# Up and down convolution on fewer weight matrices, with column-shifted copies written by ScalarE

## The chip, the cores and the metric

The kernel runs on one core of a Trainium2 chip. The metric is the device time of one launch in microseconds; the median of several launches counts. TensorE (PE) multiplies, VectorE (DVE), ScalarE (ACT) and GpSimd (POOL) work on what it leaves in PSUM, SyncE (SP) issues DMAs. Each engine runs its own instructions in order, and semaphores tie the engines together.

## The reference

16 images of 32 x 32 pixels and 32 channels pass through a group norm, a convolution branch (added to the input), attention over the 1024 tokens of each image (added), and an expert-choice feed-forward layer (added). The change lies in the convolution branch:

```python
x = x + bias
x = jnp.repeat(jnp.repeat(x, 2, axis=2), 2, axis=3)      # up by 2
x = _conv_same(x, up_filter)                             # 12 x 12 low pass
x = jax.nn.leaky_relu(x, negative_slope=0.2) * sqrt(2)
x = _conv_same(x, dn_filter)                             # 12 x 12 low pass
x = x[:, :, ::2, ::2]                                    # down by 2
```

The filters work on each channel by itself, and both are separable; the kernel convolves along one image axis by the weights of a matrix product and along the other by adding up products over shifted data.

## The kernel before, in words

An image of a channel lies on TensorE's 128 partitions as four blocks of 32 (a block holds every fourth column, R = 4), and each partition holds 256 numbers: 32 rows `h` of JW = 8 columns `j`. A shift by one of those eight columns is a move by one `j`. Values are held as two float16 parts, high and low, so every weight matrix is multiplied three times (high x high, high x low, low x high).

`up` of image n makes four quarters of the upsampled image, each of 256 columns in PSUM (psB). A quarter t takes the weight matrices UU at index 4k - t + 6 for k = -1, 0, 1 where that index lies in 0 to 9; k is also the shift by which the image is read. k = 0 is a product of 256 columns; k = -1 and k = 1 leave out the column that falls off the edge and are products of 32 x 7 = 224 columns. That makes 1 + 1, 1 + 2, 1 + 2 and 1 + 1 matrices, so 10 matrices and 30 products, 12 of 256 columns and 18 of 224. `down` sums in one PSUM range (psA) the products of DD with the four quarters in `y`: also 10 matrices and 30 products, 12 of 256 and 18 of 224. Both go through `convolve` (line 892), unshifted products first.

The order of everything is written out by hand. `STEP` (line 133) is a list of events; in step t an event `batch(5, "up")` works on image t + 5, and so on. `schedule()` walks t from -9 to 21, and every engine walks the same list `EVENTS` and does its own part of each event. In step t stand, in this order: `prob` 0 of image t, `yQ` of t + 2, `pv` of t - 1, `prob` 1, `score` 0, `up` of t + 5, `prob` 2, in some steps work of a group of four images (`image`, `mean`, `uT`, `pool`), `shift` of t + 1, `down` of t + 4, `prob` 3 and 4, `zK` of t + 3, `tok` of t + 4. So image 4 goes through `down` in step 0, and images 0 to 3 in steps -4 to -1, where no attention runs yet.

On ACT an event of `up` is two activations out of PSUM (`y` high in float16 at line 557, `y32` at line 560), `prob` an exponential (line 587), `tok` three copies (lines 563 to 569), `yQ` one copy (line 578) whose low half DVE makes (line 752), `mean` squares (line 598), `image` two copies to float16 (line 553); `image_low` is DVE's part of the images (line 698), `y_low` POOL's (line 499). PSUM is two sets of four banks, each handed out in a ring by `place`: a unit on PE waits until the unit that had its banks has been read out.

Of the kernel before, what the change touches and what calls it, by code (L numbers as in the profile page):

```python
# [16 lines left out]
P = 128  # L17
# [23 lines left out]
HOMES = 4  # L41
SLOT = 1024
# [67 lines left out]

def span_of(n, i):

    return ((0, 2), (2, 3), (3, 4))[i] if n == G - 1 else ((0, 2), (2, 4))[i]
# [20 lines left out]
        once(-8, "xT", 3), batch(0, "prob", 0), group(6, "logit_max"), batch(2, "yQ"), batch(-1, "pv"),  # L134
# [6 lines left out]
        batch(4, "down"), once(-2, "image", 1), once(-3, "small", 2),  # L141
# [58 lines left out]
def hybrid_kernel(nc, x, bias, up_filter, dn_filter, Wq, Wk, Wv, gate_w, gate_b, weight1, weight2, out):  # L200
# [9 lines left out]
    with ExitStack() as ctx:  # L210
# [13 lines left out]
        xin = sb("xin", [P, 2, SLOT])  # L224
        biasr = sb("biasr", [P, H])
# [13 lines left out]
        y = sb("y", [P, 2, SLOT])  # L239
        w1_halves = sb("w1_halves", [P, SLOT])  # L240
# [101 lines left out]
        UU_ready, UU_copied = sem("UU_ready"), sem("UU_copied")  # L342
# [49 lines left out]

        def zV_count(n):

            return zV_loaded[n % HOMES], 16 * R * (n // HOMES + 1)

# [7 lines left out]
        def _(sp):  # L404
# [61 lines left out]
        def _(pool):  # L466
# [6 lines left out]
            nc.gpsimd.memset(pooled[:, :, :], 1.0).then_inc(fills_ready, 1)  # L473
            pool.wait_ge(power_ready, 1)
# [48 lines left out]
        def _(act):  # L523
# [20 lines left out]
            for e in EVENTS:  # L544
# [3 lines left out]
                if name == "image":  # L548
                    if n >= 2:
                        act.wait_ge(b_filled, BU["up", GB * (n - 1) - 1] + 1)  # L550
                    for i, (lo, hi) in enumerate(PIECES):
                        act.wait_ge(xin_sum, 2 * n + 1 + i)
                        nc.scalar.activation(img[n % 2][0][:, lo:hi], x_all[:, n, lo:hi], ACT.Copy).then_inc(xin_high, 1)
                if name == "up":
# [24 lines left out]
                elif name == "prob":  # L579
                    if n == 0:  # L580
                        act.wait_ge(UU_ready, 16 * 2)
                        act.wait_ge(UU_copied, 2)
# [42 lines left out]
        def _(dve):  # L625
# [19 lines left out]
            for e in EVENTS:  # L645
# [70 lines left out]
                elif name == "dnT":  # L716
# [156 lines left out]
        def _(pe):  # L873
# [15 lines left out]
            def convolve(out_cols, matrices):  # L889

                for i, (m, v, shift) in enumerate(sorted(matrices, key=lambda a: a[2] != 0)):
                    ins = nc.tensor.matmul(within(out_cols, -shift), m, within(v, shift), start=i == 0, stop=i == len(matrices) - 1)  # L892
# [18 lines left out]
            for e in EVENTS:  # L911
# [34 lines left out]
                elif name == "up":  # L946
# [6 lines left out]
                    parts = [v[:, BC * (n % GB):BC * (n % GB) + BC] for v in img[n // GB % 2]]  # L953
                    for t in range(R):
                        ins = convolve(s[:, BC * t:BC * t + BC],
                                       [(UU[:, i, R * k - t + NS - 1, :, :], parts[j], k) for k in (-1, 0, 1) if 0 <= R * k - t + NS - 1 < SPAN
                                        for i, j in ((0, 0), (0, 1), (1, 0))])
                elif name == "down":

                    pe.wait_ge(y_ready, n + 1)  # L960
                    if n == 0:
                        pe.wait_ge(a_drained, A["dnT", 0] + 1)
                    ins = convolve(s[:, 0:BC], [(DD[:, i, R * k + t + 3, :, :], y_parts[n % 2][j][:, BC * t:BC * t + BC], k) for k in (-1, 0, 1)
                                                for t in range(R) if 0 <= R * k + t + 3 < SPAN for i, j in ((0, 0), (0, 1), (1, 0))])
# [134 lines left out]
```

## Time and profile before

| | us |
|---|---|
| median of 3 runs | 368.54 (368.35 to 369.02) |
| the profiled execution | 368.35 |
| its span, first to last instruction | 366.5 |
| PE busy | 327.2 (89%) |
| DVE busy | 260.1 (71%) |
| ACT busy | 183.9 (50%) |
| POOL busy | 128.8 (35%) |

The profiled execution is the lowest of the three runs. Its time is the span and 1.85 us around it. All sums are made against the 368.35 us of that execution, which lies 0.19 us below the median. An instruction's duration in a row includes the way through the engine, so that neighbours on PE and ACT overlap; the pace of an engine is read from starts.

### The profile page before, as it was taken

To read this page: it belongs to the slowest core of one execution; us is meant where nothing else is said; L and a number is where in the kernel's file an instruction comes from. 1 tells how busy PE (TensorE), PEld (TensorE's weight loads), DVE (VectorE), ACT (ScalarE), POOL (GpSimd) and SP (SyncE) were. 2 spreads that over 40 slices of the span, in tenths; PEclk is the share of its full clock that TensorE was granted. 3 is DMA by queue.
4 is the path that set the end of the run, shared out by engine and by line. 5 is a ranking of instruction groups with operands and counts; after the bars stand their busy time and mean duration, and the time that the engine had idled before them with its cause. 6 is when DMAs were issued, how large, how long until landed. Compare 5 with 4: busy or idle time off the path is not lost.

```text
span 366.5 us, 8381 instructions
## 1 busy us (share of the span) xinstructions
PE 327.2 (89%) x3362; PEld 249.3 (68%) x3362; DVE 260.1 (71%) x523; ACT 183.9 (50%) x251; POOL 128.8 (35%) x96
## 2 busy tenths in 40 slices
PE   2289998799999999999899999999996986979985
PEld 1168886587777878786678787777774544546774
DVE  2679779957757877869686876776988786454632
ACT  1043355446557574757663755576564547440500
POOL 6134535332444337554211557312235400351000
PEclk9999999999999999999999999999999899995655
DMA  4910100001011010101000101011021100100122
GB/s 125 204 36 3 26 19 16 16 16 31 16 18 26 5 32 2 31 4 32 15 16 2 31 15 17 17 16 26 7 58 32 31 2 18 28 2 29 57 75 69
DMA packets 35906, 11.16 MB, mean 30 GB/s; under 512 B 24431, under 2 KB 35741, under 8 KB 35869
## 3 DMA queue, kind: packets, MB, share of 16 engines
q1 hardware_dynamic: 33152, 9.98, 11.3%
q10 hardware_dynamic: 2717, 0.66, 1.2%
q8 instruction: 27, 0.44, 0.5%
q14 instruction: 10, 0.08, 0.1%
HBM read 5.72 MB, written 4.21 MB: 27 GB/s over the span
## 4 chain that ended last, share of the span: by engine, by line
PE 77%; DVE 10%; DMA 5%; issue 3%; ACT 2%; POOL 1%; ACTq 1%; SPq 0%; DVEq 0%; POOLq 0%
PE psB L892 14%; PE psA L892 13%; PE psB L1025 9%; PE psB L1005 8%; PE psA L990 7%; PE psA L1070 4%; PE psA L882 3%; PE psA L1048 3%; PE psB L1039 3%; DVE negmax L757 2%; PE psA L993 2%; PE psA L983 2%; PE psA L1032 2%; PE psB L1008 2%; PE psB L977 2%
## 5 line engine op out<-in xcount | busy, mean ns | idle before, releaser
L757 DVE TENSOR_REDUCE negmax<-psA 128x1 f32<-128x512 f32 (+7 forms) x128 | 90.5, 751 | 32.2 <-PE psA L993 31.6
L587 ACT ACTIVATE Pp<-psB 128x1024 f32<-128x1024 f32 (+1 forms) x80 | 73.6, 937 | 35.3 <-PE psB L1008 30.7
L892 PE MATMUL psB<-xin,UU 128*128 128x224 f16 (+1 forms) x480 | 56.4, 277 | 0.1
L892 PE MATMUL psA<-y,DD 128*128 128x224 f16 (+1 forms) x480 | 55.1, 273 | 0.0
L990 PE MATMUL psA<-zK,yQ 128*128 128x512 f16 (+1 forms) x192 | 47.8, 332 | 6.0 <-DVE uT L775 2.4
L892 PEld LDWEIGHTS psB<-xin,UU 128*128 128x128 f16 x480 | 47.0, 99 | 7.9 <-DVE xin L698 0.5
L1005 PE MATMUL psB<-yQ,zK 128*128 128x512 f16 (+1 forms) x192 | 47.3, 330 | 3.7 <-DMA yQ<-rows 2.4
L892 PEld LDWEIGHTS psA<-y,DD 128*128 128x128 f16 x480 | 46.7, 98 | 5.5
L477 POOL TENSOR_TENSOR zrstd<-zrstd,power 128x8 f32<-128x8 f32 x16 | 27.2, 1698 | 53.9 <-DVE zrstd L735 53.9
L557 ACT ACTIVATE y<-psB 128x1024 f16<-128x1024 f32 x16 | 16.4, 1023 | 44.8 <-PE psB L892 44.8
L499 POOL TENSOR_TENSOR y<-y 128x1024 f16<-128x1024 f32 x16 | 34.1, 2132 | 9.8 <-ACT y L560 9.8
L1025 PEld LDWEIGHTS psB<-Pp,zV 128*32 128x32 f32 x1024 | 26.7, 110 | 14.1 <-ACT centred L569 4.8
L1025 PE MATMUL psB<-Pp,zV 128*32 128x256 f32 (+7 forms) x1024 | 35.5, 288 | 0.5 <-ACT centred L569 0.4
L477 POOL TENSOR_TENSOR urstd<-urstd,power 128x16 f32<-128x16 f32 (+1 forms) x9 | 23.6, 2624 | 33.4 <-DVE urstd L801 33.4
L1008 PE MATMUL psB<-ident_b,mask_b 128*128 128x128 bf16 x128 | 28.1, 220 | 0.0
L1005 PEld LDWEIGHTS psB<-yQ,zK 128*128 128x128 f16 x192 | 16.9, 98 | 15.3 <-issue 3.2
L993 PE MATMUL psA<-mask_b,ident_b 128*128 128x128 bf16 x128 | 25.9, 222 | 0.0
L505 POOL COPY z<-z 128x512 f16<-128x512 f16 x16 | 9.8, 609 | 44.8 <-DVE z L748 44.8
L990 PEld LDWEIGHTS psA<-zK,yQ 128*128 128x128 f16 x192 | 16.8, 100 | 12.1 <-DVE uT L775 3.3
L511 POOL TENSOR_TENSOR u<-t_all,nmean 128x512 f32<-128x512 f32 (+1 forms) x8 | 7.9, 992 | 42.5 <-PE psA L1048 24.8
L573 ACT ACTIVATE zK<-psB 128x1024 f16<-128x1024 f16 x16 | 16.4, 1027 | 12.2 <-PE psB L977 12.2
L752 DVE TENSOR_TENSOR yQ<-psA,yQ 64x1024 f16<-64x1024 f32 x16 | 19.6, 1228 | 2.7 <-ACT yQ L578 2.4
(158 smaller groups left out, 504.5 us busy)
## 6 DMA issues: line engine op xcount, KB each, us to landing
x_all<-in_x_dram SPq DMA_DIRECT2D x4, 512.0 KB, 3.9
normalised_tokens<-z SPq DMA_DIRECT2D x16, 128.0 KB, 1.8
zV<-normalised_tokens SPq DMA_DIRECT2D x64, 32.0 KB, 2.1
out_dram<-x_all SPq DMA_DIRECT2D x8, 256.0 KB, 2.3
yQ<-rows SPq DMA_DIRECT2D x32, 2.0 KB
Pp<-filter_tables ACTq DMA_DIRECT2D x4, 121.9 KB, 3.7
w_halves<-y SPq DMA_DIRECT2D x12, 32.0 KB, 1.8
cst<-shape_constants SPq DMA_DIRECT2D x1, 326.5 KB, 4.3
```

Source lines behind the costliest of these rows:

```text
L477: return nc.gpsimd.tensor_tensor(v, v, power[:, 0:1].broadcast_to([P, n]), ALU.pow)
L499: nc.gpsimd.tensor_tensor(low, y32[:, :], high, ALU.subtract).then_inc(y_ready, 1)
L557: nc.scalar.activation(y_parts[n % 2][0], slot(e), ACT.Prelu, scale=1.0 / UP_SCALE, alpha=SLOPE)
L587: nc.scalar.activation(Pp[:, n % 2, UOFF[e[2]]:UOFF[e[2]] + N], slot(e)[:, 0:N], ACT.Exp).then_inc(b_drained, 1)
L752: nc.vector.tensor_tensor(v, s[2 * C:P, :], v, ALU.subtract).then_inc(a_drained, 1)
L757: ins = nc.vector.tensor_reduce(negmax[:, n % 2, m - 1:m], s[:, at:at + P * m], X, ALU.max, negate=True)
L892: ins = nc.tensor.matmul(within(out_cols, -shift), m, within(v, shift), start=i == 0, stop=i == len(matrices) - 1)
L990: ins = nc.tensor.matmul(s[:, lo:hi], yQ[:, n % 3, P * (m - 1):P * m], zK[:, n % 3, lo - at:hi - at], start=True, stop=not diagonal)
L993: ins = nc.tensor.matmul(s[:, hi - P:hi], ident_b[:, :], mask_b[:, :], start=False, stop=True)
L1005: ins = nc.tensor.matmul(s[:, lo:hi], zK[:, n % 3, P * j:P * j + P], yQ[:, n % 3, P * j + lo - at:P * j + hi - at], start=True, stop=not d ...
L1008: ins = nc.tensor.matmul(s[:, lo:lo + P], mask_b[:, :], ident_b[:, :], start=False, stop=True)
L1025: ins = nc.tensor.matmul(rows, zV[:, n % HOMES, j, :], probs_j[:, :, r, :], start=j == 0, stop=j == KT - 1, skip_group_check=True)
```

## The change

For images 2 to 15, ACT writes a copy `mixed` of both parts of the image (two activations of 64 partitions, 2 x 32 x 7 numbers each): partitions 0 to 63 moved by one column one way, 64 to 127 by one column the other way. In quarters 1 and 2 the matrices for k = -1 and k = 1 are nonzero in different halves of the partitions, so with that copy one matrix does for both: 8 matrices and 24 products. The matrix is UU with a piece of the other side written into rows that were zero (`filter_wrap`, two more DMAs). Images 0 and 1 (`PLAIN_UP`) go on with 30 products, and the k = 1 products of their quarters 1 and 2 read 64 partitions instead of 128. In the same way ACT writes `y_mixed` for every image, and `down` takes 9 matrices and 27 products; one more DVE copy fills DD's last slice. GpSimd clears both new tiles once at the start.

On ACT the copies of image t + 5 come in step t behind the exponential of `prob` 0, and PE waits for them ahead of `up`; the copies of y come ahead of `down` in the list, so behind the exponential of `prob` 2 and behind `image` or `mean` where the step has one, and PE waits for them after the first 24 products of `down`.

```diff
+def mixture(ahead):
+
+    return lambda t: ("mixed", t + ahead) if PLAIN_UP <= t + ahead < B else None
...
-        once(-8, "xT", 3), batch(0, "prob", 0), group(6, "logit_max"), batch(2, "yQ"), batch(-1, "pv"),
+        once(-8, "xT", 3), batch(0, "prob", 0), mixture(5), group(6, "logit_max"), batch(2, "yQ"), batch(-1, "pv"),
...
-        batch(4, "down"), once(-2, "image", 1), once(-3, "small", 2),
+        batch(4, "y_mixed"), batch(4, "down"), once(-2, "image", 1), once(-3, "small", 2),
...
+            for r in (R - 2, R - 1):
+                place_to, place_from = filter_wrap(r)
+                sp.dma_start(place_to, place_from).then_inc(UU_wrapped, 16)
...
+            nc.gpsimd.memset(mixed[:, :, :, :, :], 0.0).then_inc(mixed_zero, 1)
+            nc.gpsimd.memset(y_mixed[:, :, :, :, :], 0.0).then_inc(mixed_zero, 1)
...
+                if name == "mixed":
+                    if n < PLAIN_UP + 2:
+                        act.wait_ge(mixed_zero, 1)
+                    else:
+                        act.wait_ge(b_filled, BU["up", n - 2] + 1)
+                    act.wait_ge(xin_ready, 2 * (n // GB) + min(n % GB, 1) + 1)
+                    for to, v in mixture_halves(n):
+                        nc.scalar.activation(to, v, ACT.Copy).then_inc(mixed_ready, 1)
+                if name == "y_mixed":
+                    if n == 0:
+                        act.wait_ge(mixed_zero, 2)
+                    act.wait_ge(y_ready, n + 1)
+                    if n >= 2:
+                        act.wait_ge(a_filled, A["down", n - 2] + 1)
+                    for to, v in y_mixture_halves(n):
+                        nc.scalar.activation(to, v, ACT.Copy).then_inc(y_mixed_ready, 1)
...
+                    link(ins)
+                    ins = nc.vector.tensor_copy(DD[2 * C:P, :, SPAN - 1, 0, :], D_parts[2 * C:P, :, 0, :])
                     ins.then_inc(a_drained, 1)
...
+                    if n >= PLAIN_UP:
+                        pe.wait_ge(UU_wrapped, 16 * 2)
+                        pe.wait_ge(mixed_ready, 2 * (n - PLAIN_UP) + 2)
...
+                        if 1 <= t <= 2 and n >= PLAIN_UP:
+                            outer = [(UU[:, i, R - t + NS - 1, :, :], both[j], 0) for i, j in ((0, 0), (0, 1), (1, 0))]
+                        else:
+                            outer = [(UU[0:rows, i, R * k - t + NS - 1, :, :], parts[j][0:rows], k)
+                                     for k, rows in ((-1, P), (1, 2 * C if 1 <= t <= 2 else P)) if 0 <= R * k - t + NS - 1 < SPAN
+                                     for i, j in ((0, 0), (0, 1), (1, 0))]
...
+                    pe.wait_ge(y_mixed_ready, 2 * n + 2)
+                    both = [y_mixed[:, n % 2, j, :, :].rearrange("p h j -> p (h j)") for j in range(2)]
+                    ins = convolve(s[:, 0:BC], [(DD[:, i, SPAN - 1, :, :], both[j], 0) for i, j in ((0, 0), (0, 1), (1, 0))], first=False)
```

On PE, the products from `tok` of image 0 to `up` of image 2 stood like this before (lines 968 and 970 are `tok`, 892 is `convolve`, the first tile is the target):

```order
L968 MATMUL psB<-cst,tF 128x128 x2
L970 MATMUL psB<-cst,tF 128x128 x2
L892 MATMUL psB<-xin,UU 128x256 x3
L892 MATMUL psB<-xin,UU 128x32x7 x3
L892 MATMUL psB<-xin,UU 128x256 x3
L892 MATMUL psB<-xin,UU 128x32x7 x6
```

The same place on PE after the change (`convolve` is now line 945, `tok` 1034 and 1036), with what is waited for:

```order
L1034 MATMUL psB<-cst,tF 128x128 [waits a_drained,b_drained]
L1034 MATMUL psB<-cst,tF 128x128
L1036 MATMUL psB<-cst,tF 128x128 x2
L945 MATMUL psB<-xin,UU 128x256 [waits mixed_ready,UU_wrapped,b_drained]
L945 MATMUL psB<-xin,UU 128x256 x2
L945 MATMUL psB<-xin,UU 128x32x7 x3
L945 MATMUL psB<-xin,UU 128x256 x3
L945 MATMUL psB<-mixed,UU 128x256 x3
L945 MATMUL psB<-xin,UU 128x256 x3
```

The six shifted products of quarters 1 and 2 became three whole ones each, and `up` of image 2 now waits at its first product for copies that follow `tok` of image 0 on ACT.

On ACT, step 1 from `prob` 0 to `prob` 4, after the change (lines 595 and 603 write the copies, 638 are the exponentials, 628 `yQ`, 642 `pv`, 607 and 610 `up`):

```order
L638 ACTIVATE Pp<-psB 128x1024
L595 ACTIVATE mixed<-xin 64x64x7 x2
L628 ACTIVATE yQ<-psA 128x1024
L642 ACTIVATE oT<-psB 128x256
L638 ACTIVATE Pp<-psB 128x1024
L607 ACTIVATE y<-psB 128x1024
L610 ACTIVATE y<-psB 128x1024
L638 ACTIVATE Pp<-psB 128x1024
L603 ACTIVATE y_mixed<-y 64x64x7 x2
L638 ACTIVATE Pp<-psB 128x1024
L638 ACTIVATE Pp<-psB 128x512
```

The order of the other activations is the one of before; the four copies stand between them, the last two behind three activations of 1024 columns that all follow `up`.

## Rows read from the trace of the kernel before

**Rows 1.** The page: shares of the chain that ended last, by engine.

```profile
PE 77%; DVE 10%; DMA 5%; issue 3%; ACT 2%; POOL 1%; ACTq 1%; SPq 0%; DVEq 0%; POOLq 0%
```

**Rows 2.** Windows: stretch, its us, then busy (count) by engine, PEclk, DMA, GB/s.

```profile
36.00:71.00 35.00, 32.44 (x290) 26.89 (x290) 29.41 (x70) 15.24 (x25) 16.75 (x13) 1.00 0.08 17
71.00:137.00 66.00, 64.45 (x746) 49.69 (x746) 47.50 (x89) 42.16 (x59) 22.97 (x17) 1.00 0.10 22
...
268.00:366.50 98.50, 82.04 (x778) 56.82 (x775) 59.23 (x121) 39.80 (x53) 21.45 (x15) 0.81 0.15 37
```

**Rows 3.** Timeline (start, us, engine, line, tiles, form, count): `down` of image 7; page group.

```profile
126.34 1.47 PE L892 MATMUL psA<-y,DD 128*128 128x256 f16 x12
127.44 2.35 PE L892 MATMUL psA<-y,DD 128*128 128x256 f16 x20
L892 PEld LDWEIGHTS psA<-y,DD 128*128 128x128 f16 x480 | 46.7, 98 | 5.5
```

**Rows 4.** Lines by form, ACT: busy us and mean ns of one, idle before.

```profile
L553 ACT ACTIVATE xin<-x_all 128x768 f16<-128x768 f32 x4 | 3.4, 850 | 2.9 <-POOL x_all L487 2.9
L553 ACT ACTIVATE xin<-x_all 128x256 f16<-128x256 f32 x4 | 1.7, 423 | 1.6 <-POOL x_all L487 1.6
```

**Rows 5.** Timeline, around the starts of `down`: steps 6, 3, 0, 5, 7.

```profile
178.19 1.16 ACT L553 ACTIVATE xin<-x_all 128x256 f16<-128x256 f32 x2
176.19 0.38 PE L892 MATMUL psA<-y,DD 128*128 128x256 f16 x2
...
128.34 0.64 ACT L598 ACTIVATE sq_u<-u 128x512 f32<-128x512 f32 x1
...
79.22 1.03 ACT L587 ACTIVATE Pp<-psB 128x1024 f32<-128x1024 f32 x1
78.12 0.27 PE L892 MATMUL psA<-y,DD 128*128 128x256 f16 x1
...
159.09 1.04 ACT L587 ACTIVATE Pp<-psB 128x1024 f32<-128x1024 f32 x1
158.94 0.27 PE L892 MATMUL psA<-y,DD 128*128 128x256 f16 x1
...
198.83 0.63 ACT L598 ACTIVATE sq_u<-u 128x512 f32<-128x512 f32 x1 [2.28 <-POOL u L511]
197.55 0.27 PE L892 MATMUL psA<-y,DD 128*128 128x256 f16 x1
```

**Rows 6.** Timeline, step 3: DVE's low part of the images, ACT, `up` of image 8.

```profile
120.03 1.29 DVE L698 TENSOR_TENSOR xin<-x_all,xin 128x256 f16<-128x256 f32 x2
119.45 1.02 ACT L578 ACTIVATE yQ<-psA 128x1024 f16<-128x1024 f32 x1
122.14 3.45 PE L892 MATMUL psB<-xin,UU 128*128 128x256 f16 x30
```

**Rows 7.** Timeline, steps -3 to -1: around `up` of images 2, 3 and 4.

```profile
37.92 0.39 ACT L569 ACTIVATE centred<-psB 128x256 f32<-128x256 f32 x1
37.18 3.45 PE L892 MATMUL psB<-xin,UU 128*128 128x256 f16 x30
41.72 1.22 DVE L651 COPY xF_all<-psA 128x1024 f32<-128x1024 f32 x1
...
47.70 0.39 ACT L569 ACTIVATE centred<-psB 128x256 f32<-128x256 f32 x1
47.43 3.44 PE L892 MATMUL psB<-xin,UU 128*128 128x256 f16 x30
...
58.61 1.28 DVE L698 TENSOR_TENSOR xin<-x_all,xin 128x256 f16<-128x256 f32 x2
59.25 3.45 PE L892 MATMUL psB<-xin,UU 128*128 128x256 f16 x30
58.41 1.02 ACT L578 ACTIVATE yQ<-psA 128x1024 f16<-128x1024 f32 x1
60.46 1.23 DVE L752 TENSOR_TENSOR yQ<-psA,yQ 64x1024 f16<-64x1024 f32 x1
```

More of the change, by code:

```diff
@@ L41 @@
 HOMES = 4
+PLAIN_UP = 2
 SLOT = 1024
@@ L224, in hybrid_kernel @@
         xin = sb("xin", [P, 2, SLOT])
+        mixed = sb("mixed", [P, 2, 2, H, JW], F16)
         biasr = sb("biasr", [P, H])
@@ L239, in hybrid_kernel @@
         y = sb("y", [P, 2, SLOT])
+        y_mixed = sb("y_mixed", [P, 2, 2, H, JW], F16)
         w1_halves = sb("w1_halves", [P, SLOT])
@@ L391, in filter_place, with filter_wrap, mixture_halves, y_mixture_halves @@
                     U_parts[q, :, :, :, :].rearrange("p i m q t -> p i (m q t)"))
+        def filter_wrap(r):
+            q, n = slice(C * r, C * r + C), r - 1
+            return (UU[q, :, SPAN - n:SPAN, :, :].rearrange("p i m q t -> p i (m q t)"),
+                    U_parts[q, :, 0:n, :, :].rearrange("p i m q t -> p i (m q t)"))
+        def mixture_halves(n):
+            at = BC * (n % GB)
+            v = xin[:, n // GB % 2, :].bitcast(F16).rearrange("p (i n) -> p i n", i=2)[:, :, at:at + BC].rearrange("p i (h j) -> p i h j", j=JW)
+            return [(mixed[rows, n % 2, :, :, to:to + JW - 1], v[rows, :, :, 1 - to:JW - to])
+                    for rows, to in ((slice(0, 2 * C), 0), (slice(2 * C, P), 1))]
+        def y_mixture_halves(n):
+            v = y[:, n % 2, :].bitcast(F16).rearrange("p (i t h j) -> p i t h j", i=2, t=R, j=JW)
+            return [(y_mixed[rows, n % 2, :, :, to:to + JW - 1], v[rows, :, t, :, 1 - to:JW - to])
+                    for rows, t, to in ((slice(0, 2 * C), 2, 0), (slice(2 * C, P), 1, 1))]
         def zV_count(n):
@@ L887, in within, with convolve @@
                 return v.rearrange("p (h j) -> p h j", j=JW)[:, :, max(0, shift):JW + min(0, shift)]
-            def convolve(out_cols, matrices):
+            def convolve(out_cols, matrices, first=True, last=True):
                 for i, (m, v, shift) in enumerate(sorted(matrices, key=lambda a: a[2] != 0)):
-                    ins = nc.tensor.matmul(within(out_cols, -shift), m, within(v, shift), start=i == 0, stop=i == len(matrices) - 1)
+                    ins = nc.tensor.matmul(within(out_cols, -shift), m, within(v, shift), start=first and i == 0, stop=last and i == len(matrices) - 1)
                 return ins
@@ L952, in _ @@
                         pe.wait_ge(UU_copied, 2)
-                    parts = [v[:, BC * (n % GB):BC * (n % GB) + BC] for v in img[n // GB % 2]]
-                    for t in range(R):
+                    if n >= PLAIN_UP:
+                        pe.wait_ge(UU_wrapped, 16 * 2)
+                        pe.wait_ge(mixed_ready, 2 * (n - PLAIN_UP) + 2)
+                    of = slice(BC * (n % GB), BC * (n % GB) + BC)
+                    parts = [v[:, of] for v in img[n // GB % 2]]
+                    both = [mixed[:, n % 2, j, :, :].rearrange("p h j -> p (h j)") for j in range(2)]
+                    for t in range(R):
+                        if 1 <= t <= 2 and n >= PLAIN_UP:
[4 more added lines that the diff above has]
+                                     for i, j in ((0, 0), (0, 1), (1, 0))]
                         ins = convolve(s[:, BC * t:BC * t + BC],
-                                       [(UU[:, i, R * k - t + NS - 1, :, :], parts[j], k) for k in (-1, 0, 1) if 0 <= R * k - t + NS - 1 < SPAN
-                                        for i, j in ((0, 0), (0, 1), (1, 0))])
+                                       [(UU[:, i, NS - 1 - t, :, :], parts[j], 0) for i, j in ((0, 0), (0, 1), (1, 0))] + outer)
                 elif name == "down":
```

9 lines of the change are left out of this document (6 added, 3 removed).

## The prediction

> **What bounds the kernel now.** I read the shares of the chain first, then the busy time by stretch, then the timeline of single steps. The chain that ended last is PE for 77% of the span, ACT for 2% [rows 1]. From 71 to 137 us PE is busy 64.45 of 66 us at full clock, ACT only 42.16 [rows 2]. So in steps 0 to 10 the end is set by the order of products on PE, and a product taken out there counts in full, as long as nothing that PE waits for comes later than PE does. From 36 to 71 us, steps -4 to -1, DVE is busy 29.41 of 35 us beside PE's 32.44 [rows 2]: two engines take turns, and a late start on one is handed on by the other. So the question is not how much PE saves, but whether ACT's copies are there when PE arrives.
>
> **What is removed.** Twelve products of `down` are seen in 1.47 us and twenty in 2.35 us [rows 3]: 0.88 / 8 = 0.110 us for one more. The first are all of 256 columns, of the second 18 have 224, and the pace is the same in both. A product that replaces another is then free, and one taken away gives 0.11. `up` loses 6, 0.66 us in each of 14 images; `down` loses 3, 0.33 us in each of 16. All in all 14 x 0.66 + 16 x 0.33 = 14.5 us of PE. A rule speaks against this size. The Trainium skill (TensorE: Matmul & The Clock Gate, "Back-to-back issue gap") has the isolated gap as columns / 2.4 + 2.5 ns: 95.8 ns for 224 columns and 109.2 for 256, an estimate by that page by which whole products in place of strided ones cost something and the saving is 10.9 us. The trace disagrees: with 0.096 for a strided one the twenty would end in about 2.1 us, and it shows 2.35 [rows 3].
>
> **What a copy costs.** ACT copies 768 numbers from SBUF into float16 in 0.850 us and 256 in 0.423 [rows 4]: 0.834 ns for a number and 0.21 us fixed. A copy of the change has 2 x 32 x 7 = 448 numbers: 0.58 us. Two in a row overlap by 0.11 (these two forms in a row take 1.16, not 1.27) [rows 4, 5]. A pair so takes 1.06 us, holds ACT for 0.95, and PE's next product comes 0.10 later, the length of a weight load [rows 3]. No row has 64 partitions or runs of seven; below I let a pair be anything from 0.9 to 1.25.
>
> **`down` in steps 0 to 11.** PE reaches the 25th product 24 x 0.11 = 2.64 us after the start of `down`. ACT starts `y_mixed` only when what stands ahead is done: both activations of `up`, the exponential of `prob` 2, and `image` or `mean` if the step has one. All of that, and PE's way to `down`, hangs on the end of `up`, so a shorter `up` changes nothing in the distance. Step 0, a plain one: the exponential starts at 79.22 and takes 1.03, minus 0.11, plus 1.06 and 0.10 gives 81.30; PE arrives at 78.12 + 2.64 = 80.76 and waits 0.54 us [rows 5]. Step 6 has `image` ahead: 178.19 + 1.16 + 1.05 = 180.40 against 176.19 + 2.64 = 178.83, 1.57 us [rows 5]. Step 3 has squares ahead: 128.34 + 0.64 + 1.05 = 130.03 against 126.34 + 2.64 = 128.98, 1.05 us [rows 3, 5]. Step 5 has PE work between `up` and `down`: 161.18 against 161.58, no wait [rows 5]. Step 7 has both: 200.51 against 200.19, 0.32 us [rows 5]. The others are of these kinds, read the same way: plain 0, 1, 10 (1.45 in sum); `image` 2, 6 (3.0); squares at once 3, 4, 8 (3.15); 5, 9 none; 7, 11 (0.65). Sum 8.25 us. While PE waits, everything of the later list waits behind it on PE: `prob` 3 and 4, `score`, `zK`, `tok`, and ACT and DVE, which then wait for PE.
>
> **`mixed` in steps 0 to 10.** The copies stand ahead of `yQ` on ACT and delay that and `pv`'s copy by 0.95 us, but `pv`, `prob` 1 and `score` 0 lie between on PE, which cover it: nothing. One step differs: in step 3 the copies wait for DVE's low part of new images. Its first quarter is there at about 120.5, the pair at 121.55, `yQ` (1.02 long) ends at 122.47, `pv`'s copy at 122.74; `up` needs that bank, so it starts at 122.84 and not at 122.14: 0.7 us [rows 6].
>
> So from step 0 on: 11 x 0.66 + 12 x 0.33 = 11.2 saved, 8.25 + 0.7 = 8.95 given back, **2.3 us gained**.
>
> **Steps -4 to -1.** Here no `pv` or `prob` lies between `tok` and `up`, so the chain is PE `tok`, ACT three copies, ACT two more copies, PE `up`. Image 2: 37.92 + 0.39 - 0.11 + 1.06 + 0.10 = 39.36 against 37.18, 2.18 late, 0.66 of it made up: 1.5. PE's transposes for the next group stand behind `up`, and DVE's read of them (41.72) starts a run of DVE work on which `tok` of image 1 waits, so the 1.5 is handed on [rows 7]. Image 3: 49.14 against 47.43, 1.71 - 0.66 = 1.05 [rows 7]. Image 4: the copies need the low part, whose first quarter is there at about 59.05; `up` is 0.95 late, but made up but for 0.3; `yQ` moves to 60.0 to 61.05, and DVE, which took it at 60.46, is late by 0.6 and is the later one [rows 7]. One more DVE copy in front of `down` of image 0: 0.2. Saved products of `down` end in waits for DVE here and bring nothing. Sum **3.35 us lost**.
>
> **What else.** Images 0 and 1 have 12 products each on 64 partitions; no row shows such. From rows, a changeover can cost from nothing to a product's way through the array less its pace (1.47 - 11 x 0.11 = 0.26, less 0.11) [rows 3]: 0.15 for each of 8 changeovers, so 0 to 1.2; I take 0.3, nearer to nothing because three products of a kind stand together. The Trainium skill (TensorEngine Tiling (Array Packing), "Key Properties") says that a change of tiling mode drains TensorE, which speaks for the upper end; no run here shows it. POOL's two clears fall into its first idle time, and the two DMAs and SP's issue lie behind the two that `up` waits for now, before anything else is due: nothing.
>
> Sum: 368.35 - 2.3 + 3.35 + 0.3 = **369.7 us**. Copies of 0.9 to 1.25 a pair move about 13 waits by -0.16 to +0.19 each, so 367.6 to 372.2.
>
> **The rivals.**
> *Copies far cheaper.* If ACT wrote a pair in 0.55 us, every wait falls by 0.5: 8.25 becomes 3.8, step 3's 0.7 goes to 0.2, the start loses 1.5 less: 369.7 - 6.45 = 363.2, faster than before. It decides from about 0.95 a pair down. Against it: no ACT row is under 0.83 ns a number. Chance 0.12.
> *The start swallows its delays.* If the run of DVE in steps -3 to -1 has room that I don't see, so that `up` of images 2 to 4 is late without being on the path: 369.7 - 3.35 = 366.3. For it: DVE is 5.6 us idle there [rows 2]. Chance 0.14.
> *Waits dearer.* Short runs cost ACT more, 0.2 us a copy, so 0.4 a pair at 13 places: 374.9. A weaker form is in the tail, where the mean clock is 0.81 [rows 2]: 3 us of PE work more at half clock would cost 1.5. Chance 0.12.
> *Strided products cheaper.* If a product of 224 columns cost 224/256 of a whole one, 0.096, `up` saves 12 x 0.096 - 6 x 0.11 = 0.49 and `down` 0.25; from step 0 on that is 2.8 less, at the start 0.5: 373.0. The rows contradict it [rows 3]; chance 0.04. The gap rule of the Trainium skill named above is this case.
> *All of it counts.* If PE never waits for ACT: 368.35 - 14.5 = 353.9. The order on ACT speaks against it. Chance 0.06.
>
> **How the numbers follow.** The forecast, 367.6 to 372.2, has 0.52. About 0.2% (0.7 us) is what a measurement of this kernel can tell from no change. Of the forecast 0.31 is slower than 369.3, 0.16 within, 0.05 under 367.8; cheap copies and the full gain are faster, the start case nearly all faster (0.12 of 0.14), the two others slower. Faster 0.35, same 0.18, slower 0.47. The range leaves out the full gain, the lower half of the cheap copies and the upper part of the dear ones: 364 to 374.
>
> **What would show it.** Right: in the changed profile a wait of PE on ACT's `y_mixed` of 0.4 to 1.6 us in about nine steps, longest in steps 2 and 6, none in 5 and 9; `up` of image 2 starting some 2.2 us after its old place, ACT's copies at 0.58 us, thirty products become 24 at 0.11 us each, ACT's busy time up by some 35 us (60 x 0.58). Wrong: copies under 0.4 us; `down` running its 27 products without a gap; step 0 beginning no later than before; a pace of the whole products above 0.11 us.

## The result, and the profile after the change

The changed kernel takes 377.24 us (median of 4 runs, 372.89 to 378.91) against 368.45 us (367.96 to 369.02) on the same chip: 1.0161 times, 95% interval 1.0087 to 1.0236. Five more runs on another chip gave 378.52 us (376.28 to 379.22) against 368.70: 1.0255, 1.0231 to 1.0279. It is slower, as forecast, but by 9 us and not by 1; 377.24 lies above the range of 364 to 374. The runs of one changed kernel differ among themselves by up to 8 us, among other things by the clock of the last 98 us, and a ratio is one of means that leaves out runs over 1.5% above the fastest of their kernel (the two highest of the first four here, five of ten in e4, one of six in e12); so below, besides the times, the ends of stages ahead of that tail are compared.

The profiled execution took 378.54 us, with a span of 376.6. The page of the changed kernel, engines (busy us, share, count), granted clock in 40 slices and chain:

```profile
PE 318.9 (85%) x3230; PEld 235.7 (63%) x3230; DVE 261.9 (70%) x524; ACT 217.3 (58%) x311; POOL 129.8 (34%) x98
PEclk9999899999999999999999999999999899995655
PE 60%; ACT 13%; DVE 12%; issue 7%; DMA 5%; POOL 1%; ACTq 1%; SPq 0%; DVEq 0%; POOLq 0%
```

PE is busy 8.3 us less, and yet the span is 10.1 us longer. ACT, 2% of the chain before [rows 1], is 13% of it now, and one slice early in the program, the fifth, has a clock below 0.9. Busy time by stretch, first of the kernel before, then of the changed one (us, then busy and count of PE, PE's weight loads, DVE, ACT and POOL, granted clock, DMA share, GB/s):

```profile
36.00:73.90 37.90, 34.55 (x303) 27.89 (x304) 31.44 (x75) 17.67 (x28) 17.64 (x14) 1.00 0.08 19
73.90:268.20 194.30, 190.63 (x2147) 147.77 (x2146) 146.38 (x271) 118.13 (x162) 76.61 (x54) 1.00 0.08 17
```

```profile
36.00:83.30 47.30, 36.98 (x302) 28.14 (x300) 34.20 (x83) 27.50 (x45) 19.41 (x14) 0.96 0.07 16
83.30:278.20 194.90, 181.98 (x2043) 136.64 (x2044) 145.53 (x272) 143.23 (x207) 75.57 (x54) 1.00 0.08 17
278.20:376.60 98.40, 81.91 (x776) 57.24 (x774) 59.01 (x120) 39.80 (x53) 21.18 (x15) 0.80 0.15 37
```

The second lines run from `up` of image 5 (step 0) to the end of `down` of image 15. PE has 8.65 us less to do there, and the stretch is 0.6 us longer: all that was saved became waiting. 9.4 us were lost before step 0. The tail takes 98.4 us as before. Of what PE waited for in the changed kernel (total us, times, longest):

```profile
PE psA L945 <- ACT y_mixed L603: 8.9, 12, 1.5
PE psB L945 <- ACT mixed L595: 5.2, 3, 2.3
PE psA L1098 <- ACT oT L642: 1.0, 2, 0.5
PE psB L945 <- ACT oT L642: 0.8, 1, 0.8
```

None of these four lines exists before the change. One such wait in the timeline of step 0 (start, duration, engine, line; compare [rows 5]):

```profile
87.95 1.03 ACT L638 ACTIVATE Pp<-psB 128x1024 f32<-128x1024 f32 x1
89.00 1.18 ACT L603 ACTIVATE y_mixed<-y 64x448 f16<-64x448 f16 x2
87.00 2.79 PE L945 MATMUL psA<-y,DD 128*128 128x256 f16 x24
90.24 0.50 PE L945 MATMUL psA<-y_mixed,DD 128*128 128x256 f16 x3 [0.46 <-ACT y_mixed L603]
```

The 24 products would hand over at 87.00 + 2.62 = 89.62; the last three start at 90.24. The exponential ends at 88.98, the pair begins 0.02 later and takes 1.18. The forecast had the pair begin 0.11 before the end of the exponential and take 1.06.

### The profile page after: what moved, and what is told of

It is laid out like the page before. It is cut to its first block, busy times and chain, and to the rows that moved or that the text cites. A ratio compares the mean times of both kernels' runs of the same rounds, so it can differ in the third digit from the quotient of the medians.

```text
span 376.6 us, 8225 instructions
## 1 busy us (share of the span) xinstructions
PE 318.9 (85%) x3230; PEld 235.7 (63%) x3230; DVE 261.9 (70%) x524; ACT 217.3 (58%) x311; POOL 129.8 (34%) x98
## 4 chain that ended last, share of the span: by engine, by line
PE 60%; ACT 13%; DVE 12%; issue 7%; DMA 5%; POOL 1%; ACTq 1%; SPq 0%; DVEq 0%; POOLq 0%
PE psB L945 12%; PE psB L1091 7%; PE psA L1056 6%; PE psB L1071 6%; PE psA L1136 4%; DVE negmax L810 3%; PE psA L935 3%; ACT y_mixed L603 3%; PE psA L945 3%; PE psA L1114 3%; PE psB L1105 2%; ACT y L610 2%; ACT Pp L638 2%; PE psA L1098 2%; PE psB L1043 1%
## 5 line engine op out<-in xcount | busy, mean ns | idle before, releaser
L945 PE MATMUL psB<-xin,UU 128*128 128x256 f16 (+1 forms) x312 | 44.7, 284 | 6.3 <-ACT mixed L595 5.2
L511 POOL TENSOR_TENSOR zrstd<-zrstd,power 128x8 f32<-128x8 f32 x16 | 26.3, 1643 | 57.3 <-DVE zrstd L788 57.3
L945 PE MATMUL psA<-y,DD 128*128 128x256 f16 (+1 forms) x384 | 44.6, 273 | 0.0
L945 PEld LDWEIGHTS psA<-y,DD 128*128 128x128 f16 x384 | 37.3, 98 | 4.4
L945 PEld LDWEIGHTS psB<-xin,UU 128*128 128x128 f16 x312 | 29.8, 101 | 16.1 <-issue 8.5
```

The source lines that it names most:

```text
L511: return nc.gpsimd.tensor_tensor(v, v, power[:, 0:1].broadcast_to([P, n]), ALU.pow)
```

## The experiments

All are compared by six points read from the timeline: the start of `up` of image 0, the end of `up` of image 1, start and end of `up` of image 2, the start of step 0 (`up` of image 5) and the end of `down` of image 15; "rest" is what is left of the span. An end is the start of the last product plus 0.11. The first products of `up` of image 0 come every 0.21 us and later ones every 0.11, and where that turns differs from run to run; so that `up` takes 3.97 us in e1 and 4.55 before, and 4.28 (e6) to 5.52 (e7) where it has products of 64 partitions, and landmarks behind it can differ between two runs by about 1 us for no cause in the schedule. From step 0 to the end of `down` 15 the granted clock is full in every run.

| us | up 0 | up 1 end | up 2 | up 2 end | step 0 | down 15 end | rest |
|---|---|---|---|---|---|---|---|
| before | 21.82 | 32.35 | 37.18 | 40.46 | 73.91 | 268.21 | 98.3 |
| changed | 23.92 | 35.40 | 43.02 | 47.11 | 83.30 | 278.23 | 98.4 |
| e1_clears_alone | 23.79 | 33.74 | 38.57 | 41.85 | 75.30 | 269.58 | 98.5 |
| e2_clears_late | 22.04 | 33.27 | 40.88 | 45.17 | 81.17 | 276.09 | 94.4 |
| e3_down_alone | 21.99 | 31.97 | 37.10 | 40.38 | 73.99 | 273.64 | 98.1 |
| e4_up_alone | 22.13 | 33.70 | 40.85 | 43.47 | 82.26 | 271.62 | 98.1 |
| e5_y_early | 22.14 | 32.89 | 40.08 | 44.36 | 79.86 | 265.94 | 98.7 |
| e6_both_early | 22.00 | 32.68 | 37.39 | 40.01 | 74.52 | 261.79 | 97.7 |
| e7_plain_five | 22.05 | 35.64 | 40.77 | 44.47 | 79.16 | 274.09 | 98.4 |
| e8_half_rows | 22.23 | 33.27 | 38.10 | 41.80 | 76.08 | 274.97 | 98.5 |
| e9_fill | 22.33 | 34.21 | 41.83 | 44.45 | 82.15 | 277.13 | 98.6 |
| e10_whole_pairs | 22.28 | 34.17 | 41.38 | 44.00 | 78.94 | 270.14 | 98.5 |
| e11_after_again | 24.05 | 35.81 | 43.42 | 47.15 | 83.71 | 278.62 | 98.6 |
| e12_both_again | 21.98 | 33.17 | 37.88 | 40.50 | 75.00 | 262.28 | 94.4 |
| e13_same_half | 21.84 | 32.85 | 40.04 | 44.31 | 79.24 | 270.32 | 98.1 |
| e14_whole_again | 22.03 | 33.18 | 40.39 | 44.54 | 79.61 | 270.83 | 98.1 |
| e15_late_again | 21.73 | 32.79 | 40.41 | 44.70 | 80.70 | 275.65 | 97.8 |

**The clears.** Two kernels: the kernel before with nothing added but the two clears, and the changed kernel with the clears held back until DVE's first copies are done.

```diff
             nc.gpsimd.memset(pooled[:, :, :], 1.0).then_inc(fills_ready, 1)
+            nc.gpsimd.memset(mixed[:, :, :, :, :], 0.0)
+            nc.gpsimd.memset(y_mixed[:, :, :, :, :], 0.0)
```

```diff
+            pool.wait_ge(masks_ready, 3)
             nc.gpsimd.memset(mixed[:, :, :, :, :], 0.0).then_inc(mixed_zero, 1)
```

> The kernel before, with the two GpSimd clears of the new tiles added where the change has them, and nothing else (nobody reads the tiles). Theory A (the clears hold up DVE's first copies, and with them the filter tables): DVE's copy into pads takes some 2.3 us instead of 0.43, the transfer of the tables is issued at about 8.1 us instead of 6.3, up of image 0 starts about 2.1 us later than at 21.8, and the whole is at 370 to 371 us. Theory B (the clears fall into idle time, as the prediction had it): 368.5 us, up of image 0 at 21.8.

> The change, with the two clears held until DVE has made its first copies. Theory A: up of image 0 starts at 21.8 to 22.0 and every step lies some 2 us earlier than in the change, 371 to 376 us by the state of the tail's clock. Theory B: as the change.

e1 took 370.21 us against 368.61 (1.0041, 1.0026 to 1.0056), e2 375.99 (1.0179, 1.0130 to 1.0228). DVE and POOL at the start, of the changed kernel and then of e2:

```profile
5.63 2.34 DVE L690 COPY pads<-dnrow 32x12 f32<-32x12 f32 x1 [5.63 <-DMA dnrow<-in_L_conv_dn_filter_dram]
6.11 0.94 POOL L506 MEMSET mixed<- 128x1024 f16 x1
7.00 0.94 POOL L507 MEMSET y_mixed<- 128x1024 f16 x1
```

```profile
5.75 0.43 DVE L691 COPY pads<-dnrow 32x12 f32<-32x12 f32 x1 [5.75 <-DMA dnrow<-in_L_conv_dn_filter_dram]
6.51 0.96 POOL L507 MEMSET mixed<- 128x1024 f16 x1 [0.35 <-DVE ident_h L695]
7.40 0.95 POOL L508 MEMSET y_mixed<- 128x1024 f16 x1
```

A copy of 12 numbers a partition takes 2.34 us instead of 0.43 and ends with the second clear (7.97 and 7.94). The filter tables wait for that copy and `up` of image 0 for the tables: it starts 2.0 us late in e1, 2.1 in the changed kernel and 0.2 in e2. Without the changed convolutions 1.4 of that is left at the end of `down` 15 (e1); the other 0.6 is `up` of image 0 itself, of which less lies at the slow pace in e1. With the changed convolutions the clears cost 278.23 - 276.09 = 2.1, and 3.0 by e11 and e15. The Trainium skill (SBUF — State Buffer, "SBUF: two separate sides") says that GpSimd and a DVE instruction in a mode that uses two ports share a port pair which one of them holds for a whole instruction while the other blocks; the rows agree in that DVE is held up, here through both clears.

**One convolution alone**, both with late clears: e3 has the 27 products of `down` and the old `up` (first diff, and `mixture` and the two DMAs left out), e4 the 24 products of `up` and the old `down` (second diff, and DD's last DVE copy left out).

```diff
-PLAIN_UP = 2
+PLAIN_UP = B
```

```diff
-        batch(4, "y_mixed"), batch(4, "down"), once(-2, "image", 1), once(-3, "small", 2),
+        batch(4, "down"), once(-2, "image", 1), once(-3, "small", 2),
...
-                    pe.wait_ge(y_mixed_ready, 2 * n + 2)
```

> Only the down convolution changed (27 products and the copies of y), the up convolution as before, clears late. Theory A (PE waits for the copies of y in 10 of 12 steps, some 9.5 to 10 us in sum, against 16 x 0.33 = 5.3 us of products saved): 372.5 to 373.5 us, waits of 0.6 in plain steps, 1.3 behind squares, 1.7 behind images. Theory C (the loss is at the start and in the clock, the waits in the steps are covered by others): 363 to 367 us.

> Only the up convolution changed (24 products for images 2 to 15 and the copies of the images), the down convolution as before, clears late. Theory A (costs at the start only: waits for the copies before up of images 2, 3 and 4, some 0.4 us for each image whose products read 64 partitions; from step 0 on 11 x 0.66 us gained less 0.8 in step 3): step 0 some 5 us later than before, then 6.5 us won back, 366 to 368 us, 369.5 if the clock falls at the start. Theory D (the copies also cost in the steps, by what they delay on ACT): above 371 us.

e3: 374.54 us (1.0170, 1.0150 to 1.0190); e4: 370.70 (the median of all ten; 1.0001, 0.9969 to 1.0032). e3 comes to step 0 with no delay and then loses 5.4 us by the end of `down` 15, in which `down` saves 12 x 0.33 = 4.0: the waits are dearer than the products taken out, and the time lies 1 us above what was expected. e4 is 8.4 us late at step 0 and 3.4 at the end: it makes up 4.9 of its 11 x 0.66 = 7.3 us. Of the 8.4 us, 3.2 are the clock, which falls twice in e4 before step 0; `up` of images 3 and 4 take 4.29 and 4.16 us there and not 2.62. Without that the 5 us expected at the start are there; in the steps less is won than the 6.5 expected.

```profile
52.60:56.00 3.40, 3.40 (x18) 2.41 (x17) 1.23 (x1) 0.75 (x1) 1.37 (x1) 0.50 0.02 5
66.20:69.70 3.50, 3.24 (x16) 2.28 (x17) 2.48 (x4) 1.14 (x2) 1.64 (x1) 0.51 0.02 5
```

**Copies earlier on ACT**, late clears in both: e5 has `y_mixed` ahead of `up` in the list; e6 has besides `mixed` of the image after next there, except for the first image of a group.

```diff
-    return lambda t: ("mixed", t + ahead) if PLAIN_UP <= t + ahead < B else None
+    return lambda t: ("mixed", t + ahead) if PLAIN_UP <= t + ahead < B and ((t + ahead) % GB == 0) == (ahead == 5) else None
...
-        group(6, "logit_exp"), batch(5, "up"), once(13, "w1", 0), group(7, "wT"), batch(0, "prob", 2),
+        group(6, "logit_exp"), batch(4, "y_mixed"), mixture(6), batch(5, "up"), once(13, "w1", 0), group(7, "wT"), batch(0, "prob", 2),
...
-        batch(4, "y_mixed"), batch(4, "down"), once(-2, "image", 1), once(-3, "small", 2),
+        batch(4, "down"), once(-2, "image", 1), once(-3, "small", 2),
```

That is e6; e5 has neither the first change nor `mixture(6)`.

> The change with clears late, and the copies of y moved in the list from ahead of down to ahead of up of the same step, where ACT stands idle for some 2.7 us until up is done. Theory A (the waits of PE inside down are what the steps give back, some 9.9 us): no wait for y_mixed from step 0 on, down of image 15 ends some 9 to 10 us earlier than in e2_clears_late, at 266 to 267 us of the span; 365 to 368 us in all, since the start keeps its loss of some 7 us. Theory E (ACT has no room: the copies then delay the read-out of up, or wait for GpSimd's low part): less than half of that.

> As e5_y_early, and the copies of the images made one step earlier too, ahead of up of the image before, except for the first image of each group of four. Theory A (the start loses by PE waiting for copies behind tok on ACT, and by the clock that falls behind such a wait): up of images 2 and 3 starts within 1.2 us of its place in the kernel before, no stretch of half clock before step 0, up of image 5 starts 2 to 3 us late instead of 7.3, and the whole is 359 to 362 us. Theory F (another engine becomes the bound once PE has less to do: DVE, 71% busy): 363 us or more, with PE waiting for DVE in the steps.

> The version with both pairs of copies earlier on ScalarE and late clears, unaltered, beside the changed kernel on one chip. 361 to 364 us, 0.98 to 0.988 of the kernel before; the end of down of image 15 at 261.8 us within 0.5. A ratio of 0.99 or above would say that its gain hung on the chip that it ran on.

e5: 366.54 us (0.9952, 0.9933 to 0.9972). e6: 362.39 (0.9837, 0.9817 to 0.9858); again on another chip (e12) 360.20 (0.9771, 0.9727 to 0.9815). So this version beats both kernels; e6 lies a little above the time expected (359 to 362), e12 below its own (361 to 364). The waits for `y_mixed` are gone, and of those for `mixed` one of 1.0 us is left. ACT and PE of e6 around `down` of image 4, and its busy time from step 0 to the end of `down` 15:

```profile
75.28 1.18 ACT L604 ACTIVATE y_mixed<-y 64x448 f16<-64x448 f16 x2
76.49 1.18 ACT L596 ACTIVATE mixed<-xin 64x448 f16<-64x448 f16 x2
78.07 2.79 PE L946 MATMUL psA<-y,DD 128*128 128x256 f16 x24
80.69 0.49 PE L946 MATMUL psA<-y_mixed,DD 128*128 128x256 f16 x3
74.50:261.80 187.30, 181.07 (x2046) 137.30 (x2045) 147.80 (x270) 143.19 (x206) 76.46 (x53) 1.00 0.08 18
```

The 24 products take 2.62 us from start to start and the last three follow at once. The stretch takes 187.3 us instead of 194.3: 7.0 of the 11.2 us that were taken out; where the other 4.2 went was not followed. e5, with `mixed` at its old place, takes 186.1 us for the stretch: moving `mixed` paid at the start (step 0 at 74.52 and not 79.86), not in the steps. The copies hold ACT as long as in the changed kernel (143 us busy); they now run while PE is in `up`, for whose end ACT waited in the kernel before anyway:

```profile
ACT y L557 <- PE psB L892: 44.8, 16, 4.0
```


**Where the late start lies.** e7 leaves 30 products for images 0 to 4 (`PLAIN_UP = 5`), late clears. e8 is the kernel before in which the k = 1 products of quarters 1 and 2 read 64 partitions in all 16 images, and nothing else is changed.

```diff
-PLAIN_UP = 2
+PLAIN_UP = 5
```

```diff
-                                       [(UU[:, i, R * k - t + NS - 1, :, :], parts[j], k) for k in (-1, 0, 1) if 0 <= R * k - t + NS - 1 < SPAN
-                                        for i, j in ((0, 0), (0, 1), (1, 0))])
+                                       [(UU[0:rows, i, R * k - t + NS - 1, :, :], parts[j][0:rows], k)
+                                        for k, rows in ((-1, P), (0, P), (1, 2 * C if 1 <= t <= 2 else P)) if 0 <= R * k - t + NS - 1 < SPAN
+                                        for i, j in ((0, 0), (0, 1), (1, 0))])
```

> The change with clears late and images 0 to 4 on 30 products (the second products of 64 partitions) instead of 0 and 1. Theory A: without the waits of up of images 2, 3 and 4, and with some 0.45 us for the 64-partition products of each, up of image 5 starts some 2.5 to 3 us after its place in the kernel before, instead of 7.3; no half clock before step 0; from there the step losses of the change as they are, down of image 15 at some 272 us. Theory G (the loss at the start is from elsewhere): up of image 5 at 80 us or later.

> The kernel before, with the k = 1 products of quarters 1 and 2 of up on 64 partitions instead of 128, in all 16 images (the other rows of those weights are zero). Theory A (each change between products of 128 and of 64 partitions costs TensorE about 0.1 us, 0.42 us an image): up takes 3.70 us instead of 3.28 in every image, 374 to 375.5 us in all. Rival (the 0.42 us in the change came from something else in images 0 and 1): 368.6 us.

e7: 373.28 us (two runs, 1.0123, 1.0085 to 1.0161). It has no `mixed` before step 0 and is still 5.3 us late there: five `up` on 64 partitions cost 2.1 of that, and a stretch of 3.4 us at half clock from 29.4 us on, in `up` of image 1, up to 1.7. The 2.5 to 3 us expected, and no half clock, were a miss: the plain form is no cure, and the clock fell with no wait for copies ahead of it. e8: 375.25 us (two runs, 1.0177, 1.0156 to 1.0197). `up` takes 3.70 us there instead of 3.28. The weight loads of one `up` of e8 (partitions x columns before the shape):

```profile
125.51 1.25 PEld L892 LDWEIGHTS psB<-xin,UU 128*128 128x128 f16 x12
126.96 0.22 PEld L892 LDWEIGHTS psB<-xin,UU 64*128 64x128 f16 x3 [0.21 <-issue]
127.40 0.55 PEld L892 LDWEIGHTS psB<-xin,UU 128*128 128x128 f16 x6 [0.21 <-issue]
```

The load of each new kind waits 0.21 us where loads otherwise follow one another, and 0.11 of that reaches the products: 4 changeovers, 0.42 us an image, 6.7 in all. The Trainium skill (TensorEngine Tiling (Array Packing), "Key Properties") says that a change of tiling mode drains TensorE and gives no price; e8 shows what the change costs here.

**The fall of the clock.** In the changed kernel PE stands still for 2.3 us ahead of `up` of image 2, and from 44.0 to 47.4 us the granted clock is half:

```profile
43.02 1.21 PE L945 MATMUL psB<-xin,UU 128*128 128x256 f16 x9 [2.32 <-ACT mixed L595]
...
44.66 0.85 PE L945 MATMUL psB<-xin,UU 128*128 128x256 f16 x3
44.00:47.40 3.40, 3.40 (x19) 2.51 (x17) 1.02 (x3) 0.00 (x0) 0.61 (x1) 0.50 0.11 39
```

That `up` takes 4.09 us; at 2.4 GHz it takes 2.62. e9 puts nine idle products of 512 columns, which nothing reads, into the wait (late clears; PE's wait for the identity that they multiply is left out below).

```diff
-FILL = {("experts", 0): 5, ("turned", 0): 2, ("scatter", 1, 0): 3}
+FILL = {("experts", 0): 5, ("turned", 0): 2, ("scatter", 1, 0): 3, ("up", 2): 9}
```

> The changed kernel with late clears, and nine products of 512 columns that nothing reads (about 0.21 us each, 1.9 in all) ahead of PE's wait for the copies of image 2, which was 2.3 us long at 38.6 to 40.9 us. Theory: the half clock that followed that wait (41.5 to 44.9 us, up of image 2 4.3 us long) came from PE standing still. Then up of image 2 starts at the same 40.9 us, takes 2.6 to 2.7 us, no stretch of half clock is left between 38 and 48 us, and step 0 begins some 1.6 us earlier than with late clears alone (about 79.5 instead of 81.2 us); the time falls by 1 to 2 us from 376. Rival: the fall has nothing to do with the wait; then up of image 2 still takes over 4 us and step 0 begins at 81 us or later.

e9: 376.97 us (1.0225, 1.0211 to 1.0239).

```profile
39.35 2.10 PE L952 MATMUL psB<-ident_h 128*128 128x512 f16 x9
41.83 1.14 PE L946 MATMUL psB<-xin,UU 128*128 128x256 f16 x9 [0.38 <-ACT mixed L596]
53.43 2.02 PE L946 MATMUL psB<-xin,UU 128*128 128x256 f16 x9 [1.89 <-ACT mixed L596]
53.50:56.90 3.40, 3.40 (x17) 2.43 (x17) 1.23 (x1) 0.83 (x1) 1.46 (x1) 0.50 0.00 0
```

With the fill `up` of image 2 runs at 2.4 GHz and takes 2.62 us; but the same 3.4 us at half clock come after the next wait, that for image 3, and nothing is gained: step 0 is at 82.15, 1.0 later than in e2, of which 0.9 was there at the end of `up` 1, ahead of the fill. The theory held for the place and failed for the time. Nor does the stretch always come at a wait, nor only there: in e10 below PE waits 2.04 us at the same place, and there is none before the tail; in e4 `up` of image 2 stays at full clock behind a wait of 2.16 us; in the changed kernel the wait for image 3, 1.89 us as in e9, has none behind it; and e7 has one without such a wait. That the wait for image 2 brings the half clock is so not shown; what it costs where it comes, 1.5 us, is.

**Two copies in a row.** In e10 and e14 each copy of a pair covers 128 partitions, in e13 both cover the lower 64, and in all three the second goes to a slot of its own that nothing reads; so the products read other numbers in part of the partitions, while their order and sizes are those of e2. e15 is e2 again, on the chip of e13 and e14.

```diff
-            return [(mixed[rows, n % 2, :, :, to:to + JW - 1], v[rows, :, :, 1 - to:JW - to])
+            return [(mixed[:, n % 2 + 2 * to, :, :, to:to + JW - 1], v[:, :, :, 1 - to:JW - to])
                     for rows, to in ((slice(0, 2 * C), 0), (slice(2 * C, P), 1))]
```

`y_mixed` is changed in the same way; e13 has `0:2 * C` in place of the first colon of both tiles.

> The changed kernel with late clears in which each copy of a pair covers all 128 partitions, the second in a slot that nothing reads, so that TensorE multiplies the wrong numbers in one half of the copies; the products and their order are the same. Theory that the half of the partitions is what keeps the second copy from overlapping the first: the second starts about 0.11 us before the first ends, a pair takes 1.05 us. Rival, the reading of short runs of seven or the same tile: the pair stays at 1.18 us, the second starting 0.02 us after the first ends. A single copy takes 0.58 us either way.

> The changed kernel with late clears in which both copies of a pair cover partitions 0 to 63, the second in a slot that nothing reads; the upper half of the copies stays zero, so that TensorE multiplies zeros there. Theory that the move from one half of the partitions to the other keeps the second copy from overlapping the first: a pair takes 1.05 us, the copy after the exponential still starts late or not, and down of image 15 ends near 270 us as with whole copies. Rival, that an activation of 64 partitions never overlaps another: a pair takes 1.18 us, and down of image 15 ends near 276 us as with late clears alone.

> The copies on all 128 partitions once more, for an interval: a pair takes 1.05 us, down of image 15 ends at 270 us within 1, the time is 370 to 371, and 5 to 6.5 us below late clears alone on the same chip. If the lost overlap were not what costs, the time would be within 2 us of it.

> The changed kernel with late clears, unaltered, beside the two others on one chip: a pair takes 1.18 us, down of image 15 ends at 276 us within 1, the time is 374 to 377, spread by the clock of the tail.

e10: 370.52 us (one run); e14: 370.42 (1.0061, 1.0046 to 1.0076); e13: 370.24 (1.0075, 1.0048 to 1.0101); e15: 375.18 (1.0192, 1.0156 to 1.0229). The pair of step 0 for `mixed`, the copy behind it, and PE's waits, in e15, then e14, then e13:

```profile
79.38 1.18 ACT L596 ACTIVATE mixed<-xin 64x448 f16<-64x448 f16 x2
80.58 1.02 ACT L629 ACTIVATE yQ<-psA 128x1024 f16<-128x1024 f32 x1
PE psA L946 <- ACT y_mixed L604: 8.9, 12, 1.5
PE psA L1099 <- ACT oT L643: 1.0, 2, 0.5
```

```profile
78.41 1.03 ACT L596 ACTIVATE mixed<-xin 128x448 f16<-128x448 f16 x2
79.34 1.01 ACT L629 ACTIVATE yQ<-psA 128x1024 f16<-128x1024 f32 x1
PE psA L946 <- ACT y_mixed L604: 6.1, 8, 1.4
```

```profile
78.04 1.03 ACT L596 ACTIVATE mixed<-xin 64x448 f16<-64x448 f16 x2
78.97 1.00 ACT L629 ACTIVATE yQ<-psA 128x1024 f16<-128x1024 f32 x1
PE psA L946 <- ACT y_mixed L604: 6.0, 8, 1.3
```

With one half moved after the other, the second copy starts 0.02 us after the first has ended, in all 30 pairs, and so does `yQ` behind them; with both copies on the same partitions, 64 or 128, each starts about 0.1 before its forerunner ends. It is the move between the halves that costs the overlap, not the number of partitions or the runs of seven. Nor is it the slot that the two copies of a pair share in e15: `yQ`, which lies elsewhere, loses the overlap too. The copies on the lower half show it too. Of the 28 first copies of a pair in the changed kernel that follow their forerunner with no other wait, 16 start 0.02 us after it has ended, and each time the last activation that read SBUF was the upper copy of the pair before; the other 12 overlap, and each time that activation started at partition 0 (images, squares, logits or their exponentials). Step 6 of the changed kernel is one of the 12, where `lg` reads its bias from SBUF (compare step 0 above, with 88.98 and 89.00):

```profile
177.15 1.11 ACT L659 ACTIVATE lg<-psB,gb_sb 64x1024 f32<-64x1024 f32 x1 [1.24 <-PE psB L1105]
...
179.02 1.02 ACT L638 ACTIVATE Pp<-psB 128x1024 f32<-128x1024 f32 x1
179.94 1.17 ACT L595 ACTIVATE mixed<-xin 64x448 f16<-64x448 f16 x2
181.13 1.02 ACT L628 ACTIVATE yQ<-psA 128x1024 f16<-128x1024 f32 x1
```

So what counts is the half that ACT read or wrote last in SBUF, and not the neighbour alone. One pair thus holds ACT for 1.2 us and not for 0.93, and that is worth 275.65 - 270.83 = 4.8 us by the end of `down` 15 (5 to 6.5 were expected of the time). The Trainium skill (ScalarE: Activation LUTs, "What ACT_TABLE_LOAD costs") has activations in a row overlap by about 93 ns; e13 and e14 agree, and the pairs of the change do not.

**The changed kernel again.**

> The changed kernel unaltered, beside the others on one chip. What its runs differed by before (372.9 to 378.9 us) I put down to the clock in the last 98 us, not to the schedule: the end of down of image 15 is again at 278 us within 0.5, whatever the time; the time is 373 to 379. If the schedule varied, that landmark would move as well.

`down` of image 15 ends at 278.62 us, 0.4 from the first time. But the two profiled runs took 378.54 and 379.10 us, so this does not yet show that the landmark stays where the time moves. Other pairs of one kernel do: e2 and e15 end `down` 15 at 276.09 and 275.65 with profiled runs of 372.42 and 375.31 us, e6 and e12 at 261.79 and 262.28 with 361.38 and 358.63. The profiled runs of e2 and e12, both near the lowest of their kernels, lack a stretch of 13.7 us at half clock that the first profile of the changed kernel has (first row; the second is the whole tail of e2):

```profile
337.50:351.20 13.70, 13.69 (x68) 8.29 (x65) 6.66 (x14) 2.58 (x4) 2.95 (x3) 0.50 0.13 38
```

```profile
276.10:370.50 94.40, 77.50 (x776) 55.37 (x773) 58.97 (x120) 39.83 (x53) 21.14 (x15) 0.87 0.16 39
```

The tail of e2 takes 94.4 us at a mean clock of 0.87, that of the changed kernel 98.4 at 0.80 (row above). So 4 us of what these two differ by is the clock of the tail, and no part of the schedule. No low run of the changed kernel has a profile; its mean clock (0.966 at 372.89 us, 0.944 at 378.54) points the same way.

## Why the prediction was off, step by step

At the end of `down` 15 the forecast was a delay of -2.3 + 3.35 + 0.3 = 1.35 us; it is 10.0. The tail adds 0.1, so the whole miss lies ahead of it; the rows below sum to 9.9.

| step of the prediction | forecast | changed kernel | shown by |
|---|---|---|---|
| POOL's clears | 0 | 2.1 | e1, e2 |
| 64-partition products, images 0 and 1 | 0.3 | 0.84 | e8 |
| `up` of image 2: wait less saving | 1.5 | 2.1 | its rows, e14 |
| half clock behind that wait | none | 1.5 | its rows |
| from there to step 0 | 1.85 | 2.75 | e14 |
| steps 0 to 11 | -2.3 | +0.6 | e3, e5, e14 |

*The pace, right.* 24 products take 2.62 us where 30 took 3.28, whether of 256 or 224 columns, as [rows 3] had it; the rival of cheap strided products is out.

*The way the copies work, right.* PE waits for `y_mixed` in the steps that were named, longest in 2 and 6, not at all in 5 and 9, a copy takes 0.58 us as worked out from [rows 4], and ACT is busy 33.4 us longer (35 forecast). The rivals in which copies are far cheaper or all counts are out, and so is the one in which the start swallows its delays. The rival of dearer waits (374.9) lies nearest to the time but not by its reason: short runs cost ACT nothing, as the single copy of 0.58 us and the overlap in e13 say.

*The copy pair, the step that failed first.* It was priced at 1.06 us with the overlap of two copies of 128 partitions [rows 4, 5]; "No row has 64 partitions" stood beside it. It is 1.18, and the copies lose the overlap with what stands ahead of and behind them too. The waits in `down` of steps 0 to 11 sum to 9.8 us (from 24 x 0.109 after the start of `down` to the start of the last three) and not to 8.25; with the overlap, in e14, to 7.75. The size given for this in the range, "about 13 waits" moved by at most 0.19, left out that `mixed` holds ACT as well: `proj` in steps 4 and 8 now waits 0.5 us each time for `pv`'s copy, which the prediction had covered at "nothing"; in e14 those waits are gone. The wait in step 3 ahead of `up` was right (0.7, measured 0.8). In e14 the steps win 3.1 us, near the forecast 2.3; in the changed kernel they lose 0.6. Of the 8.7 us that the forecast missed by the end of `down` 15, the lost overlap is the largest part, 4.8 (e15 less e14).

*The start.* Its chain (`tok`, three copies, two more, `up`) is the one of the prediction. From the end of `up` 1 to step 0, e10, which has overlap and no low stretch, loses (78.94 - 34.17) - (73.91 - 32.35) = 3.2 us against a forecast of 3.35; the changed kernel loses 6.3, of which 1.5 are half clock and 1.6 the lost overlap, handed on as [rows 7] said.

*The clears, a failed cover.* They were put at nothing because POOL is idle there. They do fall into POOL's idle time; what was not asked is who works beside POOL and what POOL takes from that engine. The same goes for the clock: a new wait of 2 us on PE was priced by its length alone, and the half clock that stood behind it adds 1.5.

*The 64-partition products.* The bound was right (0 to 1.2), the value taken too near to nothing: 0.105 for a changeover and not 0.04. An image has 6 such products and not 12, as e8's rows show (two groups of three); the 8 changeovers were right.

So the forecast's sum nearly holds for the kernel that it described: e14, with overlapping pairs and clears out of DVE's way, runs at 1.0061 (370.42 us), against the forecast 369.7. At the end of `down` 15 it is 2.6 us late and not 1.35. In part that nearness is luck: 1.5 us at half clock and 0.5 more for the changeovers, neither in the sum, stand against 0.8 more won in the steps.

Not settled: why a move between halves takes the overlap away; what decides whether and where the clock falls before step 0; and what sets the clock of the tail.

## What to carry to other kernels

Work taken off the bounding engine counts only if the work that replaces it is ready when that engine arrives: look for the place in the helper's order where it waits anyway, and put the new work there (e6: 1.6 to 2.3% faster with the same instructions, in another order and with late clears, that made the kernel 2% slower). Price a form of instruction that no row shows, another set of partitions above all, by its effect on both neighbours in its queue, and measure it if the sum hangs on it. A fill by an idle engine is not free for that alone: look at what the engines beside it do at that moment, and whether their instructions get longer.

## What the runs showed of the hardware

- An activation on partitions 64 to 127 behind one on 0 to 63 starts 0.02 us after its forerunner ends, and not 0.1 before; so does one that starts at partition 0 where ACT last read or wrote SBUF from partition 64 on. Copies that all start at partition 0, on 64 or on 128 partitions, overlap.
- Two GpSimd clears in a row, of 1024 float16 numbers a partition each, held up a small float32 copy of DVE until the second was done: 2.34 us instead of 0.43.
- A change between products on 128 and on 64 partitions costs 0.105 us each way.
- Behind PE's wait of 2.3 us stood 3.4 us at 1.2 GHz; with the wait filled they stood behind the next one. Other runs had such waits without them, and one had them without such a wait.
